# Storing and loading the first head group ahead of the rest, with a new row order in the score operands

## The reference

```python
mod = silu(c) @ wmod                      # sa, ca, ga, sb, cb, gb per sequence; the gates ga, gb get |.| >= 0.25
h = layernorm(x) * (1 + ca) + sa
# attention, 16 heads of 8 features
scores = Q @ K.T / sqrt(8) + lam * (tanh(Q) @ J_h) @ tanh(K).T
probs = softmax(causal(scores))
x = x + ga * ((probs @ V) @ Wo.T + bo)
h = layernorm(x) * (1 + cb) + sb
# 8 experts, one per token by argmax(h @ centroids.T), alpha = sigmoid of the best score
y = h + relu(layernorm_e(h) @ W1[e].T + b1[e]) @ W2[e].T + b2[e]
x = x + gb * (alpha * y + (1 - alpha) * h)
```

## Time and profile before

| | us |
|---|---|
| median of 3 runs | 768.01 (767.84 to 768.46) |
| the profiled execution | 766.36 |
| its span, first to last instruction | 764.6 |
| PE busy | 674.6 (88%) |
| DVE busy | 543.4 (71%) |
| ACT busy | 501.0 (66%) |
| POOL busy | 256.5 (34%) |

### The profile page before, as it was taken

The page is one execution under the profiler, slowest core; times in us unless marked ns, Lnnn a source line. Parts: engine busy times, 40 slices in busy tenths (PEclk is TensorE's granted clock), DMA queues, the critical chain, the costliest instruction groups (busy, mean ns, idle before and its releaser), DMA issues.

```text
span 764.6 us, 15275 instructions
## 1 busy us (share of the span) xinstructions
PE 674.6 (88%) x5199; PEld 340.2 (44%) x5199; DVE 543.4 (71%) x1248; ACT 501.0 (66%) x1182; POOL 256.5 (34%) x340
## 2 busy tenths in 40 slices
PE   3657899999999998999999989999998989898693
PEld 2353333433333443443434334343443326887693
DVE  6959767877866687778667878778877802798553
ACT  1431578766768866677777676767676788657572
POOL 2009109300201842523129334120261301356643
PEclk9867699999999999999999999999999999999998
DMA  8997731446524250927604347537131464532510
GB/s 228 312 206 249 133 68 56 141 94 119 118 54 74 71 180 2 175 61 164 122 19 126 124 80 133 103 114 167 39 102 46 169 205 116 154 100 85 151 33 10
DMA packets 55444, 89.87 MB, mean 118 GB/s; under 512 B 10257, under 2 KB 26157, under 8 KB 55112
## 3 DMA queue, kind: packets, MB, share of 16 engines
q1 hardware_dynamic: 49308, 78.22, 41.7%
q0 software_dynamic: 3392, 7.90, 3.0%
q10 hardware_dynamic: 2668, 2.78, 1.3%
HBM read 50.07 MB, written 36.86 MB: 114 GB/s over the span
## 4 chain that ended last, share of the span: by engine, by line
PE 58%; DVE 17%; ACT 12%; issue 6%; DMA 4%; POOL 1%; ACTq 0%; DVEq 0%; SPq 0%; POOLq 0%
PE PS L1237 15%; PE PS L1197 13%; PE PS L1263 12%; ACT arenaA L1019 8%; DVE PS L1682 6%; PE PS L1314 4%; PE PS L1325 4%; DVE block_max L1689 3%; PE PS L1267 2%; ACT arenaB L937 2%; PE PS L1202 2%; DVE arenaB L1360 2%; PE PS L1145 1%; DVE arenaA L1360 1%; PE PS L1134 1%
## 5 line engine op out<-in xcount | busy, mean ns | idle before, releaser
L1019 ACT ACTIVATE arenaA<-PS 128x512 f32<-128x512 f32 (+3 forms) x768 | 332.5, 497 | 156.5 <-PE PS L1267 119.1
L1682 DVE CUSTOM_DVE_ANT_0 PS<-PS,mask 128x1024 f32<-128x1024 f32 (+3 forms) x256 | 261.3, 1035 | 90.2 <-PE PS L1197 87.2
L1263 PE MATMUL PS<-arenaA 99*128 99x512 bf16 (+3 forms) x768 | 221.5, 332 | 14.7 <-ACT arenaA L1019 11.6
L1197 PE MATMUL PS<-arenaA 96*128 96x512 bf16 (+3 forms) x768 | 198.7, 335 | 26.0 <-DVE maxima L1682 8.2
L1263 PEld LDWEIGHTS PS<-arenaA 99*128 99x128 bf16 x768 | 71.6, 97 | 202.2 <-ACT arenaA L1019 143.3
L1237 PE MATMUL PS<-arenaA,Vs 128*9 128x512 f32 (+3 forms) x1536 | 158.4, 488 | 0.0
L1689 DVE TENSOR_REDUCE block_max<-PS 128x8 f32<-128x1024 f32 (+1 forms) x96 | 100.3, 1045 | 28.8 <-PE PS L1202 27.8
L1197 PEld LDWEIGHTS PS<-arenaA 96*128 96x128 bf16 x768 | 66.7, 100 | 91.0 <-DVE maxima L1682 31.9
L1267 PE MATMUL PS<-after,identb 128*128 128x128 bf16 x512 | 104.5, 221 | 0.0
L836 POOL DMA_INDIRECT out_dram<-arenaA x46 | 46.0, 1000 | 80.6 <-DVE arenaA L1360 76.1
L1068 ACT ACTIVATE arenaA<-PS,b1p 128x128 f32<-128x128 f32 x184 | 52.8, 374 | 26.8 <-PE PS L1314 26.8
(11 more groups left out here) (220 smaller groups left out, 687.9 us busy)
## 6 DMA issues: line engine op xcount, KB each, us to landing
arenaA<-k_parts SPq DMA_DIRECT2D x96, 128.0 KB, 7.3
o_raw<-OT SPq DMA_DIRECT2D x32, 256.0 KB, 2.2
k_parts<-arenaB SPq DMA_DIRECT2D x24, 256.0 KB, 3.9
arenaA<-q_parts SPq DMA_DIRECT2D x16, 384.0 KB, 4.9
arenaA<-by_expert SPq DMA_DIRECT2D x31, 192.5 KB, 2.7
q_parts<-arenaB SPq DMA_DIRECT2D x18, 256.0 KB, 3.6
arenaA<-in_L_ffn_W_dram SPq DMA_DIRECT2D x2, 2048.0 KB, 13.0
arenaA<-q_parts SPq DMA_DIRECT2D x16, 256.0 KB, 5.5
```

The costliest lines, as they stand in the source:

```text
L1019: a.activation(PT[:, u % EB, h, off:HALF], PS[:, 4 + n % SB_, off:HALF], ACT.Exp).then_inc(exp_ok, 1)
L1197: last = mm(PS[:, place + c0 // HALF, at:at + c1 - c0], SQ(g, h)[0:KROWS, t * P:(t + 1) * P], SK(g, h)[0:KROWS, c0:c1], start=(at == 0), s ...
L1263: last = mm(bank[:, off:HALF], SK(g, h)[0:MROWS, kb * P:(kb + 1) * P], SQ(g, h)[0:MROWS, qc * HALF + off:(qc + 1) * HALF], start=True, sto ...
L1682: v.tensor_tensor_reduce(out=src, in0=src, in1=mask[:, S - n:S], scale=1.0, scalar=-3e38, op0=ALU.add, op1=ALU.max, accum_out=maxima[:, pl ...
```

## The change: what it does

- `load_term` takes the place of the loads by block. A term's 16 rows go to partitions t, t + 6, t + 12, ... in place of partitions 16 t to 16 t + 15, on both sides. Each side of a group is loaded by six transfers of 16 partitions: 12 transfers for a group, where there were 9. The matmuls contract over the same 96 partitions.
- `store_first` stores four heads (group 0) of each part of sequence 0 first, and the other twelve heads in a second round, which SP issues for all four tensors.
- Group 0's key side is loaded by SP once its key stores are out; its query side by SP (terms 0, 2, 4) and by ACT (terms 1, 3, 5), each after waiting for the first query stores.
- W2 is loaded behind SP's first query terms, in place of right behind W1.
- POOL waits for both rounds of stores.
- PE turns the eight pieces of W1 behind the projections and the first two chunks, as before, and the eight of W2 behind chunks 13 to 20 (`W2_FROM`), in place of chunks 2 to 9.
- SP stores the second half of the turned weights after the maxima of group 0.

The diff, without its first hunk, which only declares the semaphores `first_q_out` and `first_k_out`:

```diff
--- before.py
+++ after.py
...
@@ -388,6 +388,23 @@
         row_tile = lambda t: PAY[:, t, 0:D]
 
+        PART_OF = ((0, 1, 2, 0, 1, 0), (0, 0, 0, 1, 1, 2))
+
+        def load_term(queue, b, g, side, t):
+
+            queue.dma_start(stacks[t:KROWS:TERMS, g, side, :, :],
+                            (q_parts, k_parts)[side][bass.ds(b, 1), g * HG:(g + 1) * HG, PART_OF[side][t], :, :].rearrange("a h r q -> (a r) h q"))\
+                .then_inc(stack_in[g], 16)
+
+        FIRST_HEADS = ((0, HG), (HG, H))
+
+        def store_first(queue, n, heads, done):
+
+            k, dst, off = TENSORS[n]
+            h0, h1 = heads
+            for j in range(3):
+                queue.dma_start(dst[0, h0:h1, j, off:off + HD, :], T16[h0 * HD:h1 * HD, k, j, :]).then_inc(done, 16)
+
         @block.sync
         def _(sp):
             sp.dma_start(X[:, 0:TB, :], x[0].rearrange("(t p) d -> p t d", p=P)).then_inc(x_in[0], 16)
@@ -404,16 +421,11 @@
             ones(0)
             ones(1)
             sp.dma_start(W1r.rearrange("p (e c) d -> p e (c d)", e=E), W1.rearrange("e (p c) d -> p e (c d)", c=FC)).then_inc(w1_in, 16)
-            sp.dma_start(Aap[:, 20480:24576].rearrange("p (e f) -> p e f", e=E), W2.rearrange("e d n -> d e n")).then_inc(w2_in, 16)
-            Q_ROWS = ((0, 0, 3), (3, 0, 2), (5, 0, 1))
-            K_ROWS = ((0, 0, 1), (1, 0, 1), (2, 0, 1), (3, 1, 1), (4, 1, 1), (5, 2, 1))
 
             def load_side(b, g, side):
-                src, terms = ((q_parts, Q_ROWS), (k_parts, K_ROWS))[side]
-                for t, j, n in terms:
-                    sp.dma_start(stacks[t * ROW:(t + n) * ROW, g, side, :, :],
-                                 src[bass.ds(b, 1), g * HG:(g + 1) * HG, j:j + n, :, :].rearrange("a h j r q -> (a j r) h q"))\
-                        .then_inc(stack_in[g], 16)
+
+                for t in range(TERMS):
+                    load_term(sp, b, g, side, t)
 
             def load_group(b, g):
                 load_side(b, g, 0)
@@ -450,22 +462,29 @@
 
             for n in (1, 2):
-                k, dst, off = TENSORS[n]
                 sp.wait_ge(split0_ok, POS0[n] + 1)
-                for j in range(3):
-                    sp.dma_start(dst[0, :, j, off:off + HD, :], T16[:, k, j, :]).then_inc(parts0_k, 16)
-            sp.wait_ge(parts0_k, PARTS_OUT // 2)
+                store_first(sp, n, FIRST_HEADS[0], first_k_out)
+            sp.wait_ge(first_k_out, PARTS_OUT // 2)
             load_side(0, 0, 1)
-            sp.wait_ge(parts0_q, PARTS_OUT // 2)
-            load_side(0, 0, 0)
+            sp.wait_ge(first_q_out, PARTS_OUT // 2)
+            for t in (0, 2, 4):
+                load_term(sp, 0, 0, 0, t)
+            sp.dma_start(Aap[:, 20480:24576].rearrange("p (e f) -> p e f", e=E), W2.rearrange("e d n -> d e n")).then_inc(w2_in, 16)
+            for n in (1, 2):
+                store_first(sp, n, FIRST_HEADS[1], parts0_k)
+            for n in (0, 3):
+                store_first(sp, n, FIRST_HEADS[1], parts0_q)
             sp.wait_ge(va_ok, 1)
             load_values(0)
+            sp.wait_ge(parts0_k, PARTS_OUT // 2)
+            sp.wait_ge(parts0_q, PARTS_OUT // 2)
             load_group(0, 1)
             for k in range(2):
 
                 sp.wait_ge(w_ev, 8 * k + 8)
                 sp.dma_start(w_turned[:, k * E * FF:(k + 1) * E * FF], WTs[:, k * E * FF:(k + 1) * E * FF]).then_inc(w_out, 16)
-            send_maxima(0, T_FIRST)
+                if k == 0:
+                    send_maxima(0, T_FIRST)
             sp.wait_ge(w_out, 32)
             for g in range(2, NG):
                 ones(g)
@@ -653,6 +672,8 @@
                 g.tensor_tensor(T16[:, k, 1, :], a, zero[:, 0:1].to_broadcast([P, S]), ALU.add).then_inc(split_step, 1)
                 pool.wait_ge(split_step, done + 2)
                 g.tensor_tensor(T16[:, k, 2, :], a, T16[:, k, 1, :], ALU.subtract).then_inc(done_sem, 1)
+            pool.wait_ge(first_q_out, PARTS_OUT // 2)
+            pool.wait_ge(first_k_out, PARTS_OUT // 2)
             pool.wait_ge(parts0_q, PARTS_OUT // 2)
             pool.wait_ge(parts0_k, PARTS_OUT // 2)
             pool.sem_inc(stored, 1)
@@ -979,10 +1000,11 @@
             middle0(0)
             middle0(3)
             for n in (0, 3):
-                k, dst, off = TENSORS[n]
                 act.wait_ge(split0_ok, POS0[n] + 1)
-                for j in range(3):
-                    act.dma_start(dst[0, :, j, off:off + HD, :], T16[:, k, j, :]).then_inc(parts0_q, 16)
+                store_first(act, n, FIRST_HEADS[0], first_q_out)
+            act.wait_ge(first_q_out, PARTS_OUT // 2)
+            for t in (1, 3, 5):
+                load_term(act, 0, 0, 0, t)
             for k in range(16):
                 act.wait_ge(w_tr, k + 1)
                 src, dst = PS[:, 4 + k % 4, :], WTs[:, k * HALF:(k + 1) * HALF]
@@ -1188,7 +1210,7 @@
                 heads, t = CHUNKS[k]
                 if k == 0:
 
-                    pe.wait_ge(stack_in[g], (loads + 1) * 9 * 16)
+                    pe.wait_ge(stack_in[g], (loads + 1) * 12 * 16)
                 n = (t + 1) * P
                 for i, h in enumerate(heads):
                     place, at = bank + i // per_bank(t), i % per_bank(t) * n
@@ -1214,12 +1236,12 @@
                     last = t_.transpose(PS[:, 4 + k % 4, j * P:(j + 1) * P], W1r[:, k * 4 + j, :] if k < 8 else W2r[:, k - 8, j, :], ident[:, :])
                 last.then_inc(w_tr, 1)
 
-            turned_weights = 0
+            turned_weights, W2_FROM = 0, 13
             for i, (kind, ahead, k) in enumerate(FIRST):
                 maximum(kind, ahead, k, first_freed(i), FIRST_BANKS[i][0], 0, ahead)
                 if i == len(PREP) - 1:
                     modulations()
-                for _ in range(6 if i == len(PREP) - 1 else 1 if i >= len(PREP) and turned_weights < 16 else 0):
+                for _ in range(6 if i == len(PREP) - 1 else 1 if i >= len(PREP) + (0 if turned_weights < 8 else W2_FROM) and turned_weights < 16 else 0):
                     turn_weights(turned_weights)
                     turned_weights += 1
```

More of the change, by code:

```diff
@@ L176, in build @@
          alpha_t, alpha_ok, pay_ok, oh_ok, slots_ok, pool_step, sorted_out, sent, pads_ok, w1_in, w2_in, w_tr, w_ev, w_out, beta_in, b1_step, b1_ok, w_back,
-         tiles_ok, xsT_ps, xt_ok, w1_ok, h_ps, hr_ok, y_ps, ys_step, ys_ok, sp_turn, pads_out, ones_ok, route_chain, row_max, bias_ok, rows_step, x_stats, h_stats, moments_step, x_moments, h_moments, x_normed, h_scaled, act_used, lnt_ok, rows_made, act_turn, last_sums, last_adds, last_norms, silu3_ok, mb_ok, r1_ok, mid_ok, parts0_q, parts0_k, b1_in, first_ones) = [sem(n) for n in (
+         tiles_ok, xsT_ps, xt_ok, w1_ok, h_ps, hr_ok, y_ps, ys_step, ys_ok, sp_turn, pads_out, ones_ok, route_chain, row_max, bias_ok, rows_step, x_stats, h_stats, moments_step, x_moments, h_moments, x_normed, h_scaled, act_used, lnt_ok, rows_made, act_turn, last_sums, last_adds, last_norms, silu3_ok, mb_ok, r1_ok, mid_ok, parts0_q, parts0_k, first_q_out, first_k_out, b1_in, first_ones) = [sem(n) for n in (
             "w_in rows_in bias_in j_in consts_ok pool_chain dve_chain post_chain cols_ps cols_ok silu_e silu_ok "
@@ L182, in build @@
             "rden_out num_in at_ok h2_ok h2t_ok best_ok alpha_t alpha_ok pay_ok oh_ok slots_ok pool_step sorted_out sent "
-            "pads_ok w1_in w2_in w_tr w_ev w_out beta_in b1_step b1_ok w_back tiles_ok xsT_ps xt_ok w1_ok h_ps hr_ok y_ps ys_step ys_ok sp_turn pads_out ones_ok route_chain row_max bias_ok rows_step x_stats h_stats moments_step x_moments h_moments x_normed h_scaled act_used lnt_ok rows_made act_turn last_sums last_adds last_norms silu3_ok mb_ok r1_ok mid_ok parts0_q parts0_k b1_in first_ones").split()]
+            "pads_ok w1_in w2_in w_tr w_ev w_out beta_in b1_step b1_ok w_back tiles_ok xsT_ps xt_ok w1_ok h_ps hr_ok y_ps ys_step ys_ok sp_turn pads_out ones_ok route_chain row_max bias_ok rows_step x_stats h_stats moments_step x_moments h_moments x_normed h_scaled act_used lnt_ok rows_made act_turn last_sums last_adds last_norms silu3_ok mb_ok r1_ok mid_ok parts0_q parts0_k first_q_out first_k_out b1_in first_ones").split()]
         stack_in = [sem(f"stack_in{g}") for g in range(NG)]
```

## The result

The changed kernel takes 765.33 us (median of 7 runs, 763.91 to 766.61) against 768.01 us before (7 runs): ratio 0.9972, 95% interval 0.9959 to 0.9985. That is 2.7 us by the medians and 1.2 to 3.1 us by the interval, where 5.5 us were forecast. (The ratio is not the quotient of the two medians, which would be 0.9965; the interval holds both.) It is faster, as forecast, but the gain is about half as large.

A forecast was written before the change was run, and what follows sets the result against it. Bound at first by query stores then query loads, later by DVE's pace, in the attention by PE and DVE. Gains 6.15 + 1.0 - 1.8 + 0.3, less 0.15, taken as 5.5: 768.0 to 762.5 us, range 759.6 to 766.4.

The forecast's parts named there:

- First stores: Query stores of sequence 0: last issued at 38.05, landing after 2.9 us, out at 41.0 (40.05 to 44.84).
- rival 2: Query stores land no sooner (4 engines, key loads beside them), out at 44.8; gain about 1.8 us, 766.2; chance 0.10.
- First loads: Group 0's queries in at 45.6, first chunk on DVE at 46.5; gain 6.15 us (3.1 to 6.5).
- ACT's stand on the stores: ACT waits for query stores ahead of writing back turned weights; free at 42.3, costs nothing unless stores out later than about 41.5.
- W2's transposes: Moved within group 0's chunks: gain 1.0 us (0 to 1.2) at the beginning, loss 1.8 (0.3 to 4.4) at the end.
- The loss of 0.8: Moved W2 transposes, first chunk to first maxima: gain 1.0 us at the beginning against loss 1.8 at the end.
- POOL: Folding before the attention: starts at 58 behind the stores, ends at 78.1, hidden by 1.2 us before ACT asks at 79.3.
- the prediction's last sign: Start of the attention: if POOL ends later than ACT could begin, the forecast is wrong by that difference.
- Other groups: Three more transfers each on SP, 1.3 us of issue per group, put at nothing (within 1 us in all).
- The sum: Whole kernel: 6.15 + 1.0 - 1.8 + 0.3 = 5.65 us, less 0.15 for POOL's margins; median 762.5.
- The range: Whole kernel time from 759.6 to 766.4 us; chance 0.87 for faster.
- the forecast's own range: Whole kernel time from 761.3 to 763.8 us, around the forecast 762.5; chance 0.42.

The follow-up runs named there:

- Experiment 1: Changed kernel, but the first stores carry all 16 heads and there is no second round; ratio 0.9965 to the kernel before.
- experiment 9: Changed kernel with another HBM layout of the parts, so first stores of 32 partitions are one run of 32 equally spaced rows; ratio 0.9941 to the kernel before.
- experiment 6: Kernel before with the stores alone changed: four heads first, twelve in a second round; loads in blocks on SP; ratio 0.9993.
- experiment 2: Kernel before with only the row order changed: a term's rows on every sixth partition, twelve loads per group, all on SP; ratio 0.9974.
- second trace: Changed kernel run again unaltered on another chip; ratio 0.9972 to the kernel before, first chunk at 51.42, last maxima at 607.43.
- Experiment 4: Changed kernel with POOL's waits for the stores put behind its fold; ratio 0.9964 to the kernel before.
- second pair of traces: Kernel before and changed kernel, each run again unaltered on other chips than the result; ratios 1.0000 and 0.9972.

## Why the prediction was wrong

**First stores: the step that failed.** The prediction took "With a quarter of the bytes" a landing of 2.9 us, "the queries are out at 41.0". It took 5.37 us. Experiment 1 shows that fewer bytes win nothing by themselves (5.54 us for four times as many), the packets that only about four engines work on a four-head store (four small packets for each, where experiments 1 and 9 have 16), and experiment 9 that with the same bytes in another shape it is 2.77 us, out at 40.59, within 0.4 us of the forecast. The prediction had the rule at hand (DMA: Bandwidth & Descriptors, Why a DMA increments its semaphore by 16 and not by 1, in the Trainium skill: the number of engines divides both sides' slowest dimension) and put rival 2 on it at 0.10, with 1.8 us of gain. A chance of a tenth was far too little for it; the trace agrees with the rule's 4 engines, and with its 16 in experiments 1 and 9. Rival 2 was right in its mechanism and near in its time (766.2 against 765.33); its "stores out at 44.8" was too late by 1.3 us. That bit is the new row order's and not the split's: with the split alone the stores are out at 44.95 (experiment 6), with the row order alone at 42.57 (experiment 2). Up to there only the key loads differ from the kernel before, so it is they that left the engines sooner. The prediction's term for the stores has no part for the row order.

**First loads: a second term, mis-sized.** The new order has the data out of the way (landing 2.9 us on one queue, not 5.95; queue time 32.9% of the engines and not 41.7%). But the term "2.6 us of data, and 2.0 for issue and latency" should have been 5.86, and 6.81 in the second trace, which is what it was before (6.80). The prediction halved the 1.26 us of three issues for two queues; the change has six, three on each queue, at 0.60 us and more in place of 0.42, so the issue took 2.1 us and not 0.65 to 1.3. And the last load, split over two queues, took 4.34 us to land and not 2.9. The term also has the wrong thing for the gain: the row order alone has its queries in 6.05 us after the stores, and so have the old blocks in experiment 6; its gain is above all in the stores, which it lets out sooner. ACT's stand on the stores, costed at nothing "unless the stores are out later than about 41.5", did cost PE 2.69 us of waiting, since they were out at 43.5; the queries landed later still, so it did not decide.

These two make 46.5 into 50.33: 3.8 us, 2.5 from the stores and 1.3 from the loads.

**W2's transposes.** From first chunk to first maxima I forecast 28.4 us (74.9 - 46.5). The two traces of the changed kernel have 29.36 and 28.46, those of the kernel before 27.64 and 28.41. The loss of 0.8 is of the size seen, but so is the scatter. The mean loss of the two pairs, 0.9 us, is near the forecast by luck, for the working behind it does not hold. It reckoned the slow part of the stretch from the one place in the earlier trace rows where the clock rose during work. In the changed kernel PE worked without a gap from 63.34 on and the clock was still at 0.50 at 68, as it had been since 52; before the change it was at 1.00 from 54.8 to 68.5. So in this trace the chunks that the transposes left ran at half clock. That the clock would be up at the beginning of the attention was right in part (0.78 and, in the second trace, 0.55, for 0.51).

**POOL.** Forecast to end at 78.1, with stores out at 58; it ended at 83.72 with stores out at 63.5. W2 was issued at 45.35 and not at 42.3, which is 3.0 us of it, from the late stores and the slower issue. The other 2.5 us are a rate: the forecast moved W2 and the second round at 327 and 415 GB/s, the trace has 270 from 43.5 to 63.5. The shape of the twelve heads isn't the reason: in experiment 9, where the second round has the new shape too, POOL begins 19.7 us after the first query loads are issued, in the changed kernel 20.1. By the prediction's last sign POOL would be late by 4.4 us, but the maxima left 4.8 us late as well. Experiment 4 takes POOL's wait away and gains nothing that can be measured.

**Other groups.** At nothing, "both within 1 us in all", and nothing more is shown: from the first maxima to the last it takes 527.7 to 528.7 us in the three traces with loads in blocks and 526.9 to 528.2 in the eleven with the new rows. The means, 528.3 and 527.5, leave room for 0.8 us of gain, no more than the scatter.

**The sum.** The forecast had 5.35 us of gain at the first maxima. The trace has 0.60 (80.29 to 79.69): 3.8 us are missing at the first chunk and 1.0 between there and the maxima, of which the scatter is 0.9. At the first exponential it shows 0.87 us of gain (84.62 to 83.75), at the last maxima 1.2, by the ratio 2.2. The trace of the kernel before was of an execution 1.65 us under its median, as the prediction said; the second pair of traces has 610.26 and 607.43, 2.8 us apart. The range held the time, the forecast's own range did not.

## What to carry to other kernels

Storing only what is needed first helps only if the smaller transfer still spreads over all DMA engines: look at its slowest dimension on both sides, and at the DMA share while it is alone in flight. Here the share was 0.14 to 0.17 with stores outstanding, and mostly four packets at a time were under way on 16 engines. A transfer that moves faster also pays in what it shares the engines with: the new row order of the key loads let the query stores out 2.3 us sooner, and shortened the query loads themselves by less. Where a group of transfers waits behind another, count issues (0.6 us each here) before splitting it over queues, and check which engine's work stands behind the added wait.

## What the runs showed of the hardware

- A store whose slowest dimension is 4 heads ran on about four of the 16 DMA engines: four small packets for each store and at most six packets under way, against 16 and 18 when the same 64 KB had one dimension of 32 (the changed kernel and experiment 9). It landed 5.37 us after the last issue, against 2.77.
- Rows on every sixth partition, in place of 16 neighbours, brought the landing of a 128 KB key load in the first 130 us from 8.2 us (median before) to 2.8 with nothing else changed (experiment 2), in the direction that the port rule of the Trainium skill has (SBUF — State Buffer, Door 1: The DMA port swizzle); which ports are used no trace shows. It cost 0.17 us more at each issue (six in 3.79 us in place of 2.77).
- The same kernels took 6 to 7 us longer on the chips of the experiments, and most of it is in the experts' part: from the last maxima to the end of the span 156.65 us on the first chip and 164.0 on the other for the kernel before. What differs there wasn't looked for.
